# Second norm of an attention and feed-forward block: fp16 parts in SBUF and one DMA transpose in place of four TensorE turns

## What is computed

```python
x = x + attention(layernorm(x), ctx, ctx, q_norm_w, k_norm_w, w_out)   # 16 heads of 32, 4 key/value heads, causal
h = layernorm(x)                                                       # the second norm: 128 x 512 per batch
y = relu(h @ w_up + b_up + h @ lora_a @ lora_b)                        # 512 -> 2048, weights 4 bit, scale per 64
x = x + y @ w_down + b_down + y @ lora_a @ lora_b                      # 2048 -> 512
```

## Time and profile before

| | |
|---|---|
| median of 3 runs | 568.04 us (567.01 to 568.16) |
| the profiled execution, its own time | 565.63 us |
| its span, first to last instruction | 563.9 us |
| mean granted TensorE clock | 0.967 of 2.4 GHz |
| TensorE matmuls busy | 514.3 us, 91% of the span |
| VectorE busy | 356.2 us, 63% |
| ScalarE busy | 263.8 us, 47% |
| GpSimd busy | 205.8 us, 37% |

### The profile page before, as it was taken

How to read it: one execution, slowest core, us unless ns; L and a number is a source line. 1 busy time by engine, 2 the same in 40 slices (tenths; PEclk the granted TensorE clock), 3 DMA queues, 4 the chain that set the end, 5 groups by cost and what they waited for, 6 DMA issues and landing times.

```text
span 563.9 us, 12246 instructions
## 1 busy us (share of the span) xinstructions
PE 514.3 (91%) x4968; PEld 366.7 (65%) x4968; DVE 356.2 (63%) x674; ACT 263.8 (47%) x819; POOL 205.8 (37%) x238
## 2 busy tenths in 40 slices
PE   0257888899999999999999999999999999999997
PEld 0124445475777676767676768686868686868683
DVE  1877636554586868686868686868686868473441
ACT  1457747646453535353545454545454545343110
POOL 2493754802515151525252525252525252222100
PEclk9999559799999999999999999999999999999999
DMA  8960703101203030303030303030303020200000
GB/s 175 293 165 6 240 26 108 37 3 33 59 10 80 11 80 11 81 11 81 11 80 12 80 13 78 11 82 10 80 17 75 11 58 10 57 2 20 2 21 19
DMA packets 59769, 31.87 MB, mean 57 GB/s; under 512 B 48288, under 2 KB 50608, under 8 KB 59664
## 3 DMA queue, kind: packets, MB, share of 16 engines
q1 hardware_dynamic: 56864, 30.58, 21.4%
q10 hardware_dynamic: 2768, 0.34, 0.5%
q0 software_dynamic: 80, 0.16, 0.1%
HBM read 16.39 MB, written 4.19 MB: 37 GB/s over the span
## 4 chain that ended last, share of the span: by engine, by line
PE 82%; POOL 6%; issue 4%; DMA 2%; SPq 2%; DVE 2%; ACT 2%; POOLq 0%; DVEq 0%
PE ff L680 31%; PE ff L695 29%; PE tb L661 7%; PE tb L543 4%; PE tb L650 3%; PE sb L642 2%; DMA big<-in_L_ffn_w_up_q 2%; POOL big L334 2%; PE ff L543 2%; POOL big L331 1%; POOL pr L360 1%; PE kxb L543 1%; PE ff L588 1%; PE ff L603 1%; ACT pr L477 1%
## 5 line engine op out<-in xcount | busy, mean ns | idle before, releaser
L680 PE MATMUL ff<-xnT_hi,wu_hi 128*128 128x128 f16 x1024 | 174.0, 219 | 2.0 <-ACT wd_lo L452 1.1
L360 POOL TENSOR_TENSOR pr<-pr,rinv 128x512 f32<-128x512 f32 x64 | 78.8, 1231 | 265.3 <-DVE rinv L824 265.3
L680 PE MATMUL ff<-xnT_hi,wu_lo 128*128 128x128 f16 x1024 | 173.9, 219 | 0.0
L680 PE MATMUL ff<-xnT_lo,wu_hi 128*128 128x128 f16 x1024 | 173.9, 219 | 0.0
L695 PE MATMUL ff<-wd_hi,x 128*128 128x512 f16 x512 | 152.4, 379 | 0.0
L680 PEld LDWEIGHTS ff<-xnT_hi,wu_hi 128*128 128x128 f16 x1024 | 100.1, 98 | 14.4 <-DVE z L843 11.7
L512 ACT ACTIVATE x<-z 128x512 f16<-128x512 f32 x64 | 40.4, 631 | 133.4 <-DVE z L843 133.4
L680 PEld LDWEIGHTS ff<-xnT_lo,wu_hi 128*128 128x128 f16 x1024 | 100.2, 98 | 0.3
L680 PEld LDWEIGHTS ff<-xnT_hi,wu_lo 128*128 128x128 f16 x1024 | 100.2, 98 | 0.0
L477 ACT ACTIVATE pr<-pr,nmax 128x128 f32<-128x128 f32 x256 | 98.8, 390 | 0.0
L695 PE MATMUL ff<-wd_lo,x 128*128 128x512 f16 x256 | 97.0, 379 | 0.0
(11 more groups left out here) (135 smaller groups left out, 687.2 us busy)
## 6 DMA issues: line engine op xcount, KB each, us to landing
xt<-in_x SPq DMA_DIRECT2D x16, 256.0 KB, 3.0
big<-in_L_ffn_w_up_q SPq DMA_DIRECT2D x4, 1024.0 KB, 13.9
big<-in_L_ffn_w_down_q SPq DMA_DIRECT2D x4, 1024.0 KB, 5.3
out<-y SPq DMA_DIRECT2D x16, 256.0 KB, 2.0
kvt<-in_ctx SPq DMA_DIRECT2D x16, 64.0 KB, 2.5
wd_lo<-in_L_xattn_w_out SPq DMA_DIRECT2D x1, 1024.0 KB, 13.7
wd_hi<-in_L_ffn_w_up_lora_b SPq DMA_DIRECT2D x3, 128.0 KB, 8.7
wd_hi<-in_L_xattn_q_norm_w SPq DMA_DIRECT2D x1, 256.0 KB, 6.6
```

The costliest lines, as they stand in the source:

```text
L360: pool.tensor_tensor(pr[:, m], pr[:, m], rinv[:, p, 4 * m:4 * m + 4].unsqueeze(2).broadcast_to([P, NG, P]), ALU.mult).then_inc(probs, 1)
L680: last = pe.matmul(bank[:, P * h:P * h + P], a[:, m, cols], b[:, p, m, :], start=(h == 0 and m == 0 and i == 0), stop=(m == KC - 1 and i = ...
```

## The change

xn2 is no longer turned by TensorE. In slot 0 VectorE forms xn2 right after `hidden` (`second_norm`); ScalarE, after `split_queries` and ahead of its weights and attention work, writes the high fp16 part in the natural layout (`second_norm_high`); VectorE takes the low part (`second_norm_low`) after `centre`, ahead of `residual`, `mask_and_max` and `queries`; SyncE, after the transpose of q of the same slot, issues one DMA transpose of both parts, 128 x 1024 fp16, into `xnT` (eight 128x128 blocks). The up product waits for that transfer. `xnT` is single: the transfer waits for the up product of the batch before (`up_done`). The bank `kxb` is gone.

```diff
-        xnT_hi, xnT_lo = sb("xnT_hi", [P, 2, KC, P], F16), sb("xnT_lo", [P, 2, KC, P], F16)
+        xn_parts, xnT = sb("xn_parts", [P, 2, C], F16), sb("xnT", [P, 2 * KC, P], F16)
+        xnT_hi, xnT_lo = xnT[:, 0:KC, :], xnT[:, KC:, :]
...
# SyncE, after the transpose of q (L298)
+                n = at(s, R_NORM2)
+                if n is not None:
+                    sp.wait_ge(xn_high, n + 1)
+                    sp.wait_ge(xn_low, n + 1)
+                    if n > 0:
+                        sp.wait_ge(up_done, 4 * n)
+                    sp.dma_start_transpose(xnT[:], xn_parts[:].rearrange("p a c -> p (a c)")).then_inc(xn2_turned, 16)
...
# ScalarE: out of attention(s), slot 1; into slot 0, after split_queries(s)
-                    act.wait_ge(xn2_turned, n + 1)
-                    act.activation(xnT_hi[:, n % 2], kxb[:].rearrange("p (k t) -> p k t", k=KC),
-                                   ACT.Copy, scale=XN_SCALE).then_inc(xn_high, 1)
+            def second_norm_high(s):
+                n = at(s, R_NORM2)
+                if n is not None:
+                    act.wait_ge(xn2_ready, n + 1)
+                    if n > 0:
+                        act.wait_ge(xn2_turned, 16 * n)
+                    act.activation(xn_parts[:, 0, :], xn2[:], ACT.Copy, scale=XN_SCALE).then_inc(xn_high, 1)
...
# TensorE: out of turns(s); the wait and the operand of the up product
-                    for m in range(KC):
-                        last = turn(kxb[:, P * m:P * m + P], xn2[:, P * m:P * m + P], start=True, stop=True)
-                    last.then_inc(xn2_turned, 1)
...
-                            pe.wait_ge(xn_low, n + 1)
+                            pe.wait_ge(xn2_turned, 16 * n + 16)
...
# VectorE: out of attention_late(s); two functions of slot 0
+            def second_norm(s):
...
+                    if n > 0:
+                        dve.wait_ge(xn_low, n)
                     dve.tensor_scalar(xn2[:], x1[:, p, :], mv2[:, p, 0:1], inv2[:, p:p + 1],
                                       ALU.subtract, ALU.mult).then_inc(xn2_ready, 1)
+            def second_norm_low(s):
+                n = at(s, R_NORM2)
                 if n is not None:
                     dve.wait_ge(xn_high, n + 1)
+                    dve.scalar_tensor_tensor(xn_parts[:, 1, :], xn2[:], XN_SCALE, xn_parts[:, 0, :],
+                                             ALU.mult, ALU.subtract).then_inc(xn_low, 1)
...
                 hidden(s)
+                second_norm(s)
...
                     centre(s)
+                second_norm_low(s)
                 residual(s)
                 mask_and_max(s)
                 queries(s)
```

More of the change, by code:

```diff
@@ L33 @@
 R_PT = ((8, 15), (9, 16), (10, 17), (11, 18))
-R_PV, R_OSPLIT, R_PROJ, R_X1, R_POW2, R_NORM2, R_TURN2 = (12, 20), (13, 21), (13, 21), (14, 22), (14, 23), (15, 24), (16, 25)
+R_PV, R_OSPLIT, R_PROJ, R_X1, R_POW2, R_NORM2 = (12, 20), (13, 21), (13, 21), (14, 22), (14, 23), (15, 24)
 R_UP, R_DOWN = (18, 26), (22, 30)
@@ L153, in build @@
         tb = [bank("tb0"), bank("tb1")]
-        kxb = bank("kxb")
         norm_w_in = sem("norm_w_in")
@@ L500, in attention @@
                                        ACT.Copy).then_inc(probsT, 1)
-                n = at(s, R_TURN2)
+            def second_norm_high(s):
+                n = at(s, R_NORM2)
                 if n is not None:
-                    act.wait_ge(xn2_turned, n + 1)
-                    act.activation(xnT_hi[:, n % 2], kxb[:].rearrange("p (k t) -> p k t", k=KC),
-                                   ACT.Copy, scale=XN_SCALE).then_inc(xn_high, 1)
+                    act.wait_ge(xn2_ready, n + 1)
+                    if n > 0:
+                        act.wait_ge(xn2_turned, 16 * n)
+                    act.activation(xn_parts[:, 0, :], xn2[:], ACT.Copy, scale=XN_SCALE).then_inc(xn_high, 1)
             def hidden_high(s):
@@ L521, in _ @@
                 split_queries(s)
+                second_norm_high(s)
                 ts = tiles_at(s)
@@ L673, in feed_forward @@
                         pe.wait_ge(*up_free[n, g])
-                        bank, p = ff[up_bank[n, g]], n % 2
+                        bank = ff[up_bank[n, g]]
                         terms = ((wu_hi, xnT_hi), (wu_hi, xnT_lo), (wu_lo, xnT_hi))
@@ L679, in feed_forward @@
                                 for i, (a, b) in enumerate(terms):
-                                    last = pe.matmul(bank[:, P * h:P * h + P], a[:, m, cols], b[:, p, m, :],
+                                    last = pe.matmul(bank[:, P * h:P * h + P], a[:, m, cols], b[:, m, :],
                                                      start=(h == 0 and m == 0 and i == 0), stop=(m == KC - 1 and i == 2),
@@ L943, in attention_late @@
                     if n > 0:
-                        dve.wait_ge(xn2_turned, n)
+                        dve.wait_ge(xn_low, n)
                     dve.tensor_scalar(xn2[:], x1[:, p, :], mv2[:, p, 0:1], inv2[:, p:p + 1],
                                       ALU.subtract, ALU.mult).then_inc(xn2_ready, 1)
-                n = at(s, R_TURN2)
+            def second_norm_low(s):
+                n = at(s, R_NORM2)
                 if n is not None:
                     dve.wait_ge(xn_high, n + 1)
-                    dve.scalar_tensor_tensor(xnT_lo[:, n % 2], kxb[:].rearrange("p (k t) -> p k t", k=KC),
-                                             XN_SCALE, xnT_hi[:, n % 2], ALU.mult, ALU.subtract).then_inc(xn_low, 1)
+                    dve.scalar_tensor_tensor(xn_parts[:, 1, :], xn2[:], XN_SCALE, xn_parts[:, 0, :],
+                                             ALU.mult, ALU.subtract).then_inc(xn_low, 1)
             def result(s):
```

## The result

Four executions of the changed kernel took 610.57 to 619.90 us, median **617.61**, beside 568.10 (567.01 to 568.16) for the kernel before on the same chip: a ratio of **1.084** (95% interval 1.080 to 1.089). The forecast of 581.7 had the right side, but a loss of 13.7 us in place of 49.5, and the range ended at 596. Its mean granted clock is 0.934 (before 0.967); two of the other three have 0.934 and 0.936, and the fastest 0.955.

The account below looks back on a forecast made before the run. TensorE's list of work was taken to bound the kernel from batch 2 on. Batches 2 to 13 +13.8 us, batch 1 +0.9, batches 0, 14 and 15 together -1.0: +13.7 on 568.0 gives 581.7 us, range 569 to 596.

Parts of the forecast that it names:

- Step 1: VectorE forms xn2 right after the reciprocal, taking 0.55 us, with 1.26 as the upper end.
- xn2 stays behind GpSimd: Rival: VectorE's norm takes 1.26 us in most periods, giving 591 us; chance 0.15.
- Step 2: ScalarE's high part takes 0.60 us from SBUF; later ScalarE work moves about 0.45 us at no cost.
- Step 3: VectorE's low part takes 0.69 us, then `queries` 0.66, ending at 200.12 instead of 198.30.
- Step 4: SyncE issues q's transpose first, at 200.14 instead of 198.32; the new transpose is issued only after it.
- Step 5: The new transfer lands 4.3 + 1.3 us after q's issue; the up product starts 1.15 us later per period.
- the transfer in time: Rival: both transposes together need 1.5 us less, so all 6.7 us are gained, 561.3 us; chance 0.12.
- the one with its fixed part a second time: Rival: the new transpose lands 3.0 us after q's, +2.85 us per period, 604 us; chance 0.1.
- The turns' 0.44: Removing four turns from TensorE saves 0.44 us per batch, 6.7 us for batches 1 to 15 if nothing waits.
- Batches 14 and 15, the scores, the probabilities: Without q, batches 14 and 15 gain 0.44 and 0.5 us; scores and turns of the probabilities never wait.
- The start, bounds -1 to +1: Batch 0: high part ahead of two weight copies may cost half a us, four turns leave; taken as 0.
- the clock falls at each stall: Rival: thirteen stretches at granted clock 0.50 for 6.8 us add 44 us, giving 626 us; chance 0.03.

Follow-up runs that it names:

- doubled turns: The kernel before with each of TensorE's four turns of xn2 done twice, batches 0 to 15: 574.76 us, ratio 1.012.
- trace of after: Profiled execution of the changed kernel itself, against the kernel before: 619.9 us, span 618.1.
- filled wait: The changed kernel with ten matmuls, results unread, on TensorE ahead of the up product's wait in batches 1 to 15: 604.69 us, ratio 1.069.
- queries first: The changed kernel with VectorE's `queries` back ahead of the second norm, SyncE's order still q then xn: 562.22 us, ratio 0.995.
- queries between: The changed kernel with xn's transpose ahead of q's on SyncE and `queries` between the second norm and its low part: 567.30 us, ratio 0.999.
- bias add late: The changed kernel with GpSimd's addition x1 + bias moved from slot 0 to slot 5 of the period: 587.17 us, ratio 1.036.

## Why the forecast was right in direction and wrong in size

- **Step 1, the norm at 0.55**: right in all periods seen; the 1.26 came only with `queries` ahead of it. The rival "xn2 stays behind GpSimd" did not happen.
- **Step 2, the high part at 0.60, at no cost in a period**: 0.63, right.
- **Step 3, the low part 0.69 and then `queries` 0.66**: the low part was 0.75; `queries` was 1.75, and this is the first step that failed. I had compared the norm's place with L360's and taken care that it started ahead, but did not do the same for `queries`, which the new order puts 1.8 us later, into L387 (L395 after). Rows 5 stop ahead of that instruction, which I had not looked for, though rows 4 and 7 gave a hint of the price (1.26 for 0.55). The next row of that view shows it running at 199.46, where the forecast starts `queries`:

```profile
199.16 1.44 POOL L387 TENSOR_TENSOR y<-x,bd_bc 128x512 f32<-128x512 f32 x1
```

  Mis-sized by 1.1 us in each of 13 periods, 14 us; shown by moving the bias add, which brought 1.42 and 29.23.
- **Step 4, q issued first, and late**: right, and the two together make the change slow: with xn first, or with q first but issued early, no loss is left.
- **Step 5, the second transfer 5.6 us after q's issue**: 5.5, right. Neither the transfer in time nor the one with its fixed part a second time. What it left out is that landings vary: the 5.6 holds in seven of thirteen periods, an eighth is 0.4 late, and the other five more. That cost 1.8 us in batch 1 and 4.7 in the batches behind it. In the kernel before, q's late landings (up to 5.8 us in these periods, for a median of 4.3) cost nothing, having slack.
- **The turns' 0.44**: right, by 27.63 without waits (0.47 less) and by the doubled turns (0.4 more).
- **Batches 14 and 15, the scores, the probabilities**: nothing waited there, right.
- **The start, bounds -1 to +1**: outside the bounds in this trace, by some 7 us. The half us that I put down for ScalarE was there (0.52, in all seven traces with this order). The rest is not shown to come from the change. By 94 us the trace of after is 3 us behind, ahead of anything that the diff touches, and the kernel with the filled wait, the same code up to batch 0's up product, starts that at 109.83, 0.65 earlier than the kernel before, with 6.8 us at half clock, as before. What the change costs in the start stays open.
- **The rival "the clock falls at each stall", chance 0.03**: it happened in 8 of 13 periods, for 13.4 us. I had argued from a stretch of the start with many short waits at clock 1.00 that a fuller period was safe. That row speaks of busy time, and what came ahead of each fall here was one idle stretch. At the forecast's own stall of 1.4 to 1.6 us it was right that nothing fell, ten times out of ten. The error of step 3 carried the stall past the point. The size was also off: 3.4 us at half clock, where the rival had 6.8, and 1.3 to 1.6 us lost for each (periods less their stalls); only the first took 6.8, and lost 2.6 in the stretch counted here.

Put together, on the forecast's 13.7: + 14 for `queries`, + 6.5 late landings, + 13.4 clock, + 7 for the start of this execution make 55, against 54.2 between the spans.

## What to carry to other kernels

Where an edit moves an instruction of VectorE, set its new start against GpSimd's timeline, and do so for everything queued behind it: the one that shifts as a side effect is the one missed. Two transfers of one queue are two places in a line, so the one with the nearer deadline goes first, or the other is issued early enough; here the order in the queue alone is the difference between +8.4% and -0.7%, and the early issue alone that between +8.4% and -0.5%. Price a stall of TensorE with its clock, and compare its length with idle stretches of the trace, not with a busy share. That holds for a stream otherwise full: in the start of the kernel before, with several waits close together, the clock fell at 100.5 us with none of them longer than 1.33 us.

## What was not expected of the hardware

- `queries` and the low part, VectorE instructions with two 128x512 inputs in SBUF, that start while GpSimd runs a tensor_tensor of that size end 0.54 to 0.55 us after GpSimd's. Their price is what is left of it: the low part takes 0.75 with 0.2 us left (after), 0.98 with 0.4 (queries first) and 1.75 with 1.2 (queries between), in place of 0.69; `queries` takes 1.53 with 1.0 left and 1.75 with 1.2, in place of 0.66. The norm ends 0.28 after GpSimd's, at 1.26 in place of 0.55. Those that start a little ahead take their usual time, and so do, beside GpSimd, the reduction L922 (0.69) and L847, which reads PSUM (0.75).
- One idle stretch of TensorE is enough to halve its clock in a stream otherwise full. In the trace of after it did so behind three of the eight stalls of 2.45 to 2.89 us and behind all five of 3.2 and more; with the bias add late behind the three of 2.77 to 2.94 and none of the ten of 1.39 to 1.57. The clock then stood at 0.50 for 3.4 us. Matmuls of no use in the gap kept it up.
- A DMA transpose of 262 KB lands 3.0 us after its issue and one of 524 KB 4.3; with the smaller behind the larger, 5.5 for both, where nothing comes between.
- In some periods the flow of a transpose stops for 1.2 us. In after all six late landings had a fetch of instructions in between, and none of the seven usual ones; whether the fetch is the cause was not tried.
